# A new order for attention, FFN slots 0 and 1 filled bank by bank, and other slots for VectorE's high parts in a vision tower on one core

## What is computed

```
hx = layernorm(x);  q, k, v = hx @ Wq, hx @ Wk, hx @ Wv        # 2 heads of 64
attn = softmax(causal(l2norm(q) @ l2norm(k).T))
y = (attn @ v) @ Wo
gate = softmax(y @ gate_W + gate_b)                            # 8 experts
hid = gelu(einsum('bnd,edf->bnef', y, W1) + b1)                # 512 wide for each expert
eo = einsum('bnef,efd->bned', hid, W2) + b2
out = einsum('bned,bne->bnd', eo, gate)
```

## Time and profile before

| | |
|---|---|
| median of 3 runs | 1539.38 us (1537.39 to 1545.45) |
| the profiled execution, its own time | 1542.88 us |
| its span, first to last instruction | 1540.7 us |
| mean granted clock of TensorE | 0.986 of full speed |
| busy, share of the span | PE 1462.2 us (95%), DVE 1238.6 (80%), ACT 1082.8 (70%), POOL 329.9 (21%) |

### The profile page before, as it was taken

How to read it: one execution, slowest core, us unless ns; L and a number is a source line. 1 busy time by engine, 2 the same in 40 slices (tenths; PEclk the granted TensorE clock), 3 DMA queues, 4 the chain that set the end, 5 groups by cost and what they waited for, 6 DMA issues and landing times.

```text
span 1540.7 us, 31400 instructions
## 1 busy us (share of the span) xinstructions
PE 1462.2 (95%) x10991; PEld 994.6 (65%) x10991; DVE 1238.6 (80%) x2585; ACT 1082.8 (70%) x1861; POOL 329.9 (21%) x337
## 2 busy tenths in 40 slices
PE   7898889999999999999999999999999999999998
PEld 4554556666666666666666666666666666666665
DVE  6768798878888888888888788888788888887765
ACT  5232667777777777786777777786777777777766
POOL 1135044030121313130211313130211213130101
PEclk9998899999999999999999999999999999999979
DMA  7866053333324242434233242433333242433324
GB/s 241 202 155 140 2 164 46 101 45 100 45 61 84 27 115 39 103 42 104 42 92 53 32 113 36 109 45 100 42 94 50 47 95 34 110 44 102 54 92 55
DMA packets 40340, 125.55 MB, mean 81 GB/s; under 512 B 5744, under 2 KB 5744, under 8 KB 38128
## 3 DMA queue, kind: packets, MB, share of 16 engines
q0 software_dynamic: 22464, 55.81, 25.7%
q1 hardware_dynamic: 17696, 69.28, 12.7%
q10 hardware_dynamic: 144, 0.01, 0.0%
HBM read 68.98 MB, written 50.48 MB: 78 GB/s over the span
## 4 chain that ended last, share of the span: by engine, by line
PE 59%; DVE 22%; issue 9%; ACT 7%; DMA 2%; DVEq 1%; ACTq 0%; POOLq 0%
PE pair L1009 18%; PE pair L1028 18%; PE pair L779 6%; DVE area L1434 4%; PE pair L766 4%; DVE area L1447 3%; ACT area L645 3%; PE pair L943 3%; PE pair L931 3%; DVE mx L1332 2%; ACT area L640 2%; DVE root_t L1267 2%; PE pair L807 2%; DVE area L1347 2%; PE pair L950 2%
## 5 line engine op out<-in xcount | busy, mean ns | idle before, releaser
L640 ACT ACTIVATE area<-pair,pack_b_sb 128x680 f32<-128x680 f32 x512 | 422.6, 828 | 208.1 <-PE pair L1009 206.3
L1434 DVE TENSOR_TENSOR area<-area 128x680 f16<-128x680 f32 x512 | 458.2, 898 | 128.7 <-ACT area L645 124.1
L1028 PE MATMUL pair<-area,ws 128*128 128x340 f16 x3072 | 527.9, 308 | 15.7 <-DVE area L1447 11.8
L1009 PE MATMUL pair<-area,ws 128*128 128x340 f16 x3072 | 530.2, 308 | 1.4
L1028 PEld LDWEIGHTS pair<-area,ws 128*128 128x128 f16 x3072 | 286.4, 98 | 178.9 <-DVE area L1447 44.0
L1009 PEld LDWEIGHTS pair<-area,ws 128*128 128x128 f16 x3072 | 295.3, 98 | 144.1 <-ACT area L645 3.6
L475 POOL DMA_DIRECT2D tower_out<-area x128 | 109.9, 859 | 1030.7 <-DVE area L1447 979.7
L645 ACT ACTIVATE area<-pair,pack_b_sb 128x680 f16<-128x680 f32 x384 | 316.6, 825 | 0.0
L1447 DVE SCALAR_TENSOR_TENSOR area<-pair,pack_b_sb,area 128x340 f32<-128x340 f32 x256 | 133.6, 562 | 9.4 <-PE pair L1028 9.2
L604 ACT ACTIVATE area<-pair,nbias,root 85x85 f32<-85x85 f32 (+1 forms) x256 | 112.4, 463 | 4.2 <-DVE nbias L1335 4.2
L766 PE MATMUL pair<-area,pack_a_sb 128*128 128x392 f32 (+1 forms) x260 | 92.7, 499 | 17.5 <-DVE area L1254 14.4
(11 more groups left out here) (222 smaller groups left out, 1772.8 us busy)
## 6 DMA issues: line engine op xcount, KB each, us to landing
tower_out<-area POOLq DMA_DIRECT2D x128, 340.0 KB, 4.6
area<-gate_scratch SPq DMA_DIRECT2D x16, 1360.0 KB, 10.0
area<-gate_scratch SPq DMA_DIRECT2D x16, 1020.0 KB, 7.3
area<-cells SPq DMA_DIRECT2D x16, 392.0 KB, 4.9
area<-cells POOLq DMA_DIRECT2D x14, 392.0 KB, 6.5
area<-area POOLq DMA_DIRECT2D x14, 392.0 KB, 4.3
tower_out<-ht SPq DMA_DIRECT2D x16, 340.0 KB, 2.3
area<-gate_scratch SPq DMA_DIRECT2D x16, 340.0 KB, 4.7
```

Of the source, the lines that this page charges most:

```text
L640: nc.scalar.activation(two(hid[slot % NHID]), halves(hid_ps[slot % 2]), ACT.Gelu_apprx_tanh, bias=col(COL_B1 + slot)).then_inc(hid_ready, 1)
L1009: last = mm(hid_ps[slot % 2][:, j, 0:TH], lhs[:, w], rhs[:, j * TH:(j + 1) * TH], start=(i == 0), stop=(i == 2))
L1028: last = mm(eo_ps[:, j, 0:TH], lhs[:, w], rhs[:, j * TH:(j + 1) * TH], start=(m % CH == 0 and i == 0), stop=(m % CH == CH - 1 and i == 2))
L1434: v.tensor_tensor(hl[slot % NPART], hid[slot % NHID], hh[slot % NPART], ALU.subtract).then_inc(hlo_ready, 1)
```

## The change

Five edits.

- DVE, attention: values_out(0) stands between normalise(0) and normalise(1), and turned(0) ahead of normalise(2).
- PE, attention: `graph_of(2)` stands between turn_probs(0) and turn_probs(1), `graph_of(3)` ahead of turn_probs(3), and project(0) ahead of weigh(2).
- PE, start of the FFN: after each logits(j) come slot 0's and slot 1's matmuls of bank j (3 + 3).
- The eight high parts that DVE makes are those of slots 7, 9, 11, 14, 19, 28, 29, 31. ACT makes all others, that of slot 0 among them.
- The waits that follow from this (`hidden_read`, `his`, the count in `hhi_dve`).

```diff
+DVE_HI = (7, 9, 11, 14, 19, 28, 29, 31)
...
         def hi_on_act(slot):
 
-            return slot % CH > 0
+            return slot not in DVE_HI
...
+            def hidden_read(g, slot):
+
+                if hi_on_act(slot):
+                    pe.wait_ge(hhi_act, his(g, slot + 1))
+                else:
+                    pe.wait_ge(hid_ready, g * SLOTS + slot + 1)
...
                 if later:
-                    pe.wait_ge(hhi_act, his(g, 0) - 1 + m)
+                    hidden_read(g - 1, SLOTS - 2 + m)
...
                 graph_of(1)
                 turn_probs(g, 0)
+                graph_of(2)
                 turn_probs(g, 1)
-                graph_of(2)
                 weigh(g, 0)
                 turn_probs(g, 2)
                 weigh(g, 1)
+                graph_of(3)
                 turn_probs(g, 3)
-                graph_of(3)
+                project(g, 0)
                 weigh(g, 2)
-                project(g, 0)
                 weigh(g, 3)
...
+            def expert_half(slot, j):
+                w = slice(slot * D, (slot + 1) * D)
+                for i, (lhs, rhs) in enumerate(((w1h, yh), (w1h, yl), (w1l, yh))):
+                    last = mm(hid_ps[slot % 2][:, j, 0:TH], lhs[:, w], rhs[:, j * TH:(j + 1) * TH],
+                              start=(i == 0), stop=(i == 2))
+                return last
+
             def experts_in(g, slot):
...
+                if slot == 0:
+                    pe.wait_ge(wlo_done, 1)
+                    for j in range(2):
                         logits(g, j)
...
+                        for n in range(2):
+                            last = expert_half(n, j)
+                            if j == 1:
+                                last.then_inc(hid_ps_ready, 1)
+                if slot >= 2:
+                    hidden_read(g, slot - 2)
+                    if slot % CH == 0:
+                        pe.wait_ge(wlo_done, 2 * (slot // CH) + 1)
+                    expert_half(slot, 0)
+                    expert_half(slot, 1).then_inc(hid_ps_ready, 1)
...
                 normalise(g, 0)
+                values_out(g, 0)
                 normalise(g, 1)
-                values_out(g, 0)
                 values_out(g, 1)
+                turned(g, 0)
                 normalise(g, 2)
-                turned(g, 0)
                 turned(g, 1)
```

More of the change, by code:

```diff
@@ L303, in hi_on_act @@
         def hi_on_act(slot):
-            return slot % CH > 0
+            return slot not in DVE_HI
         def his(g, slot):
-            return g * (SLOTS - E) + len([n for n in range(slot) if hi_on_act(n)])
+            return g * (SLOTS - len(DVE_HI)) + len([n for n in range(slot) if hi_on_act(n)])
         def steps_in(slots, slot):
@@ L993, in logits @@
                 last.then_inc(logit_ps, 1)
-            def experts_in(g, slot):
[L997 to L1006, removed]
-                        logits(g, j)
[L1008 to L1011, removed]
+            def expert_half(slot, j):
[4 more added lines that the diff above has]
+                return last
+            def experts_in(g, slot):
+                if slot == 0:
+                    pe.wait_ge(wlo_done, 1)
+                    for j in range(2):
+                        logits(g, j)
+                        for n in range(2):
[8 more added lines that the diff above has]
+                    expert_half(slot, 1).then_inc(hid_ps_ready, 1)
             def experts_out(g, m):
@@ L1432, in experts @@
                     v.tensor_copy(hh[slot % NPART], hid[slot % NHID]).then_inc(hhi_dve, 1)
-                    dve.wait_ge(hhi_dve, g * E + slot // CH + 1)
+                    dve.wait_ge(hhi_dve, g * len(DVE_HI) + DVE_HI.index(slot) + 1)
                 v.tensor_tensor(hl[slot % NPART], hid[slot % NHID], hh[slot % NPART], ALU.subtract).then_inc(hlo_ready, 1)
```

## The result

| | median, us | its runs | against before |
|---|---|---|---|
| before | 1541.34 | 1537.39 to 1545.45, 6 runs | |
| after | 1563.06 | 1558.19 to 1570.58, 6 runs | 1.0146 [1.0116, 1.0176] |

The change made the kernel slower by 1.5%. The profiled execution of after took 1561.38 us (span 1559.3, mean granted clock 0.975), 18.5 more than that of before.

A forecast was written before the change was run, and what follows sets the result against it. PE's pace was taken to bound the kernel, so only its waits could be won back: -17.9 over 14 groups, -2.6 in group 0 and -1.5 in the last attention, together -22.0, giving 1517.4 us, range 1507 to 1534.

The forecast's parts named there:

- Attention, -0.66: Attention's new order on DVE and PE: logits(1) and the tanh come 0.66 us earlier in each group.
- Banks, 0 on the path: Slots 0 and 1: three more matmuls fill 0.43 of PE's wait, given back ahead of slot 2; 0 on the path.
- Slot 0's high part on ACT: FFN start: slots 2 and 3 wait for ACT, out(0) no longer for DVE; -0.66 becomes -0.30 up to out(0).
- DVE's backlog: Experts' ends: casts moved off DVE free out(4) and out(12) of their waits, -0.50 and -0.48 a group.
- I take 0 for this end: Slots 28 to 31: POOL holds slot 29's cast, PE loses 0.5 ahead of out(28), attention's waits absorb it; 0 net.
- the upper bound of 1.3: Slots 28 to 31: +1.3 a group if POOL holds both casts through a whole subtraction, less what ACT gives back.
- The rule that the prediction named: GpSimd shares SBUF interfaces with VectorE and contends with it; said to speak against high parts at slots 29 and 31.
- The clock, a rival at 0.08: FFN start: gathered waits pull PE's clock down, slots 2 and 3 lose 0.85 each, 1.7 a group; 1557 us, chance 0.08.
- a single wait of 0.88: Argument against the clock's fall: single waits of this length were followed by the full clock in each group.
- -1.28: Sum for one group of the loop: -0.30 - 0.50 - 0.48, times 14 is -17.9 us.
- 2.6 and 1.5 were to be won: Outside the loop's 14 groups: -2.6 us in group 0 (first attention and FFN 0), -1.5 in the last attention.
- 1517.4: Forecast median in us, -1.4% against a before median of 1539.38, given a chance of 0.58.

The follow-up runs named there:

- e6_banks: Before with only the new bank order of slots 0 and 1: 1547.3 us, 1.0024 of before.
- e11_old_slots: After with DVE's high parts back at slots 0, 4, 8, 12, 16, 20, 24, 28: 1531.76 us, 0.9928 of before.
- e3_fill: After with seven more matmuls, results unread, on PE ahead of slot 2: 1546.99 us, 1.0036 of before.
- e9_away_fill: After with DVE's high parts of slots 29 and 31 moved to 23 and 26, and seven unread matmuls ahead of slot 2: 1519.34 us, 0.9859 of before.
- e12_att_slots: After with the old bank order and DVE's high parts at slots 0, 7, 11, 14, 19, 23, 26, 28: 1513.82 us, 0.9811 of before.
- e4_pool_small: After with POOL's four subtractions at the FFN's end on 16 of 680 columns: 1543.58 us, 1.0006 of before.
- e1_hi_away: After with DVE's high parts of slots 29 and 31 moved to 23 and 26: 1549.24 us, 1.0041 of before.
- e8_best: After with DVE's high parts at slots 0, 7, 11, 14, 19, 23, 26, 28: 1526.15 us, 0.9887 of before.

## Why the prediction was wrong

- **Attention, -0.66: right.** From DVE's second normalise (1047.83) to logits(1) it was 11.15, forecast 11.32 (693.19 to 704.51). The first turn has no wait, turn(2) waits 0.31 for a normalise (forecast 0.3). Alone it gave -0.81 a group.
- **Banks, 0 on the path: right as a term**, shown by e6_banks and e11_old_slots. What it did to the clock belongs below.
- **Slot 0's high part on ACT, and DVE's backlog, -0.30, -0.50 and -0.48: right.** Slot 2 waited 1.12 for L646 (forecast 1.3 by starts), out(0), out(4) and out(12) not at all. From the tanh to out(27) a clean group of after took 59.95 against 60.62, -0.67, forecast -0.62 (-0.98, and the 0.36 that out(0) loses against the tanh).
- **"I take 0 for this end": the step that failed.** The working beside it had one cast held for up to 0.9 and PE losing 0.5, and set against that what ACT gives back. Measured: +1.93 in the trace, +1.86 by the slots (e3_fill against e9_away_fill), above the upper bound of 1.3. The hold of slot 29's cast was sized well (0.82: 1.34 less 0.52). What was wrong is that it stood alone and that attention would take it up. Slot 31's cast was held for 0.77 too, and the three subtractions, which had holds before, took 0.94 more in sum. PE lost 0.73 ahead of out(28), forecast 0.5, and 0.58 ahead of the values. Attention didn't take the delay up, for it begins with DVE's first normalise, and DVE had no idle time left ahead of that: it came 1.93 late, and from it to the tanh it took 14.35 (1046.24 to 1060.59), which is the length before less the 0.8 of the new order. ACT's earlier gelus gave back no more than the 1.64 of DVE's idle time that the 1.93 already counts: its exponentials are released by DVE's `nbias`, and it stood idle for 4.3. The rule that the prediction named (Trainium skill, GPSIMD Engine Reference, Specifications: contention with VectorE instructions in a two-port mode or with two SBUF inputs) agrees with these rows for the subtractions, whose two inputs are in SBUF, and for the weighing, which has one in PSUM and wasn't held; in which mode the casts run no row shows. It was weighed against the change and then priced at nothing.
- **The clock, a rival at 0.08: it happened**, at the place named (slot 3 and out(0) in the rows above, slots 2 and 3 in the rival), and at the size given for two slow slots (1.7), in every second group. That the rival's 1557 us lies so near the measured 1563.06 is luck: with falls in half of the groups it comes to some 1531, and the rest is the end of the FFN. The argument against it, a single wait of 0.88 with the full clock behind it, compared a wait by itself with three close together. The Trainium skill (TensorE: Matmul & The Clock Gate, A second HAM failure mode: psum-queue depth-cycling) has a kernel in which short idle times between groups of matmuls throttle PE again and again; the runs here show falls of this sort behind waits of 0.41 to 1.12.
- **The sum.** For a clean group: -0.81 (attention alone) and -0.67 (tanh to out(27)) with +1.93 give +0.45, and 86.21 is +0.44 over 85.77. Half the groups add 1.7, so +1.3 on average where -1.28 stood: 2.6 x 14 is 36, and with the first and last group, which show no gain (2.6 and 2.8 lost where 2.6 and 1.5 were to be won, the last in part by the clock), this makes up about the 46 between 1517.4 and 1563.06. The two ends are the weak part of this sum: 1.6 of the first 2.6 were to be won ahead of the first tanh, in a stretch that varies by 8 us.

Had the slots avoided the FFN's end and slot 0, and the banks kept their order, more than the forecast would have come: e12_att_slots, at 84.04, is -1.73 a group where -1.28 was forecast.

What stays open is why the fall comes in every second group in one kernel and in each group in another. The waits are the same in neighbouring groups of after, and e4_pool_small, whose only edit is far from them, has it in each. The pattern is a regular one, not chance: in e1_hi_away the periods repeat after five groups (85.8, 85.8, 85.8, 85.6, 87.1), in after and e11_old_slots after two, in e4_pool_small and e8_best after one.

## What to carry to other kernels

Where VectorE and GpSimd work in the same stretch, price an added VectorE instruction by what the two engines' rows look like side by side: here a VectorE instruction that met one of GpSimd's ended only behind it, so that a cast of 0.52 took 1.3 and a subtraction of 0.87 up to 2.0, and the price on the path was 1.9 for two casts. Then ask how much idle time VectorE has up to the next place where others wait for it: here it covered 1.64 of 3.57. On a PE that is 97% busy the idle time that is left is worth watching for where it gathers: a trade that moves a wait beside another one, with the sum unchanged, can cost the clock, as the order of banks did in e6_banks. Test a trade with a few useless matmuls in the wait: if that alone makes the kernel faster, as e3_fill, the clock was part of the loss.

## What the runs showed of the hardware

- Two kernels with less lost time had more falls of the clock: e1_hi_away and e4_pool_small fell in nearly each group and after in every second. A gain at one end of a group was partly paid back at the other.
- Useless work made a kernel faster: seven matmuls a group took after from 1.0146 to 1.0036 of before, three took 85.33 a group to 84.04.
- A hold works both ways. With two more casts of VectorE in that stretch, POOL's own casts took 1136 ns on average, and 888 before; its subtractions hardly changed (1636 and 1601). From the pages of before and after:

```profile
L429 POOL CAST area<-area 128x680 f16<-128x680 f32 x56 | 49.8, 888 | 39.5 <-ACT area L568 39.5
L430 POOL CAST area<-area 128x680 f16<-128x680 f32 x56 | 63.6, 1136 | 31.4 <-ACT area L569 31.4
```

VectorE's casts took 706 ns on average in the same page, and 522 before.
